# FFN tail of a gated-experts kernel: eight tiles singly and four pairs, each group's product ahead of the next transposes, and the grid subtraction shared by VectorE and TensorE

## What is computed

```python
def _quant_e4m3(t):
    amax = jnp.max(jnp.abs(t)).astype(jnp.float32)
    scale = jnp.maximum(amax / E4M3_MAX, 1e-12)
    fp8 = (t.astype(jnp.float32) / scale).astype(jnp.float8_e4m3fn)
    return (fp8, scale)
...
x = x + jnp.tanh(g_xattn[0]) * _L0_xattn_ref(_layernorm(x, axis=-1), itok_BxS_13_99985, ctx_2048, ctx_2048, ctx_2048)
x = x + jnp.tanh(g_ffn[0]) * _L0_ffn_ref(_layernorm(x, axis=-1), L0_ffn_weight)
```

## Time and profile before

| | us |
|---|---|
| median of 3 runs | 201.29 |
| lowest and highest run | 201.24, 203.76 |
| the profiled execution's own time | 201.43 |
| span of its profile | 199.7 |
| busy in the span: TensorE (PE) | 144.3 |
| VectorE (DVE) | 156.3 |
| ScalarE (ACT) | 112.7 |
| GpSimd (POOL) | 81.8 |

### The profile page before, as it was taken

The page is one execution under the profiler, slowest core; times in us unless marked ns, Lnnn a source line. Parts: engine busy times, 40 slices in busy tenths (PEclk is TensorE's granted clock), DMA queues, the critical chain, the costliest instruction groups (busy, mean ns, idle before and its releaser), DMA issues.

```text
span 199.7 us, 3062 instructions
## 1 busy us (share of the span) xinstructions
PE 144.3 (72%) x723; PEld 69.7 (35%) x727; DVE 156.3 (78%) x351; ACT 112.7 (56%) x166; POOL 81.8 (41%) x117
## 2 busy tenths in 40 slices
PE   0141939998999797999998999999851266566600
PEld 0110424443555343544444445555420223223200
DVE  2876697798758799899989787776686999998820
ACT  2366596887524854688868534233313987666510
POOL 7158787320312344332386673001110023566670
PEclk9999996999999999999999999999997579999985
DMA  0937998200000222111212210000000002132351
GB/s 6 365 113 198 355 408 264 85 2 0 0 3 0 54 56 53 26 39 43 54 26 53 56 26 0 3 0 2 0 5 0 0 0 105 57 153 113 149 208 59
DMA packets 15440, 15.68 MB, mean 79 GB/s; under 512 B 10816, under 2 KB 11328, under 8 KB 15424
## 3 DMA queue, kind: packets, MB, share of 16 engines
q1 hardware_dynamic: 12576, 7.09, 11.8%
q0 software_dynamic: 2560, 8.39, 11.6%
q10 hardware_dynamic: 288, 0.00, 0.1%
HBM read 8.92 MB, written 4.19 MB: 66 GB/s over the span
## 4 chain that ended last, share of the span: by engine, by line
PE 38%; DVE 33%; issue 11%; POOL 7%; ACT 6%; DMA 1%; DVEq 1%; POOLq 0%
PE four_ps L465 10%; PE four_ps L457 10%; PE four_ps L470 9%; DVE w_hi L1044 3%; DVE hT_hi L1052 3%; PE four_ps L498 3%; POOL x L341 3%; PE four_ps L569 2%; DVE bn L880 2%; DVE zT_lo L866 2%; DVE bn L832 2%; DVE x L1056 2%; ACT y L703 2%; DVE z L861 2%; DVE w_lo L824 2%
## 5 line engine op out<-in xcount | busy, mean ns | idle before, releaser
L364 POOL DMA_INDIRECT out<-x,token_of x16 | 19.3, 1208 | 25.4 <-DVE x L1056 22.9
L359 POOL TENSOR_TENSOR rstd<-var,minus_half 128x1 f32<-128x1 f32 x16 | 8.8, 552 | 49.3 <-DVE var L888 49.3
L633 ACT ACTIVATE zT_hi<-four_ps 128x512 f16<-128x512 f32 x19 | 11.3, 595 | 18.9 <-PE four_ps L498 18.9
L457 PE MATMUL four_ps<-w_hi,hT_hi 128*128 x76 | 21.3, 394 | 0.8 <-ACT w_hi L596 0.7
L624 ACT ACTIVATE sg<-four_ps,job_inv_a 128x512 f32<-128x512 f32 x19 | 12.9, 679 | 15.4 <-PE four_ps L470 12.4
L341 POOL DMA_INDIRECT x<-in_x,token_of x16 | 17.4, 1088 | 7.0 <-issue 4.2
L457 PE MATMUL four_ps<-w_hi,zT_hi 128*128 x76 | 19.5, 379 | 0.8 <-ACT zT_hi L633 0.8
L465 PE MATMUL four_ps<-w_lo,hT_hi 128*128 x76 | 19.9, 384 | 0.0
L615 ACT ACTIVATE w<-x,nmr,rstd 128x512 f32<-128x512 f32 x16 | 13.0, 810 | 11.9 <-DVE nmr L894 11.5
L470 PE MATMUL four_ps<-w_hi,zT_lo 128*128 x76 | 19.5, 379 | 0.0
L465 PE MATMUL four_ps<-w_lo,zT_hi 128*128 x76 | 19.5, 379 | 0.0
(11 more groups left out here) (148 smaller groups left out, 293.4 us busy)
## 6 DMA issues: line engine op xcount, KB each, us to landing
w<-in_ctx_t SPq DMA_DIRECT2D x4, 1024.0 KB, 9.4
wf<-in_wf_t SPq DMA_DIRECT2D x1, 512.0 KB, 15.4
x<-in_x,token_of POOLq DMA_INDIRECT x16, 5.9
out<-x,token_of POOLq DMA_INDIRECT x16, 2.9
hT_hi<-h_row SPq DMA_TRANSPOSE x9, 2.3
hT_lo<-h_row SPq DMA_TRANSPOSE x9, 2.3
ids_s<-in_ids SPq DMA_DIRECT2D x1, 8.0 KB, 2.9
g_s<-in_g_x ACTq DMA_DIRECT2D x1, 0.5 KB, 2.7
```

What stands on the lines that cost most here:

```text
L364: pool.indirect_dma_start(out, bass.IndirectOffsetOnAxis(ap=token_of[:, i:i + 1], axis=0), block_of(x1, i), None, bounds_check=T - 1).then ...
L457: pe.matmul(ps, lhs_hi(k), w_block(w_hi, expert, k), start=(k == 0), stop=False)
```

## The change

- `FIRST` makes twelve groups: tiles 0, 1, 2, 3, pairs {4,5}, {6,7}, {8,9}, {10,11}, then 12, 13, 14, 15.
- Transposes go to four f32 banks, `q_ps`, one a tile (tile i to bank i mod 4), and `r_ps`, `c_ps`, `n_ps`, `m_ps` become names of these. The transposes are ordinary matmuls against the identity in place of `pe.transpose`.
- `split(g)` says who subtracts. VectorE rounds tiles 0, 1, 3, 4, 6, 8, 10, 13, 15 as before. For tiles 2, 5, 7, 9, 11, 12, 14 TensorE does it as it transposes: four bf16 matmuls of vm against minus the identity, and four f32 matmuls of vt against the identity, summed in PSUM.
- TensorE issues the transposes of g, waits for their copy, issues the product of g, and only then the transposes of g+1.
- ScalarE scales three groups ahead in place of four, and `to_bf16(g)` follows `copy_qT(g)` in the same turn.
- `max_second` of tile 14 stands ahead of the two end reductions instead of behind them.
- GpSimd makes `minus_ident` at the start; VectorE's `grid` waits for `qT_done` in place of `q8_done` where the ring is used again.

```diff
-        FIRST = [0, 1, 2, 4, 6, 8, 10, 12, 14, 15, TILES]
+        FIRST = [0, 1, 2, 3, 4, 6, 8, 10, 12, 13, 14, 15, TILES]
...
+        q_ps = psum("q_ps", [P, 4 * D], F32)
+        r_ps, c_ps, n_ps, m_ps = [q_ps[:, n * D:(n + 1) * D] for n in range(4)]
...
+        def split(g):
+
+            tiles = list(tiles_of(g))
+            return (tiles[:1], tiles[1:]) if g in (0, GROUPS - 1) or g % 2 or len(tiles) > 1 else ([], tiles)
...
+            pool.tensor_scalar(minus_ident[:, :], ident[:, :], -1.0, None, ALU.mult).then_inc(pool_const, 1)
...
+            def transposed(g):
+
+                by_dve, by_pe = split(g)
+                if reused(g, 4):
+                    pe.wait_ge(qT_copied, reused(g, 4))
+                if by_pe:
+                    pe.wait_ge(vt_done, g + 1)
+                for i in by_pe:
                     for k in range(K):
-                        mm = pe.transpose(qT_ps[g % NQ][:, n * D + k * P:n * D + (k + 1) * P],
-                                          q8[:, i % NB, k * P:(k + 1) * P], ident_bf[:, :])
+                        pe.matmul(q_block(i, k), vm[:, i % NB, k * P:(k + 1) * P], minus_ident[:, :],
+                                  start=(k == 0), stop=False)
+                    for k in range(K):
+                        mm = pe.matmul(q_block(i, k), vt[:, i % NB, k * P:(k + 1) * P], ident[:, :],
+                                       start=False, stop=(k == K - 1))
+                if by_dve:
+                    pe.wait_ge(q8_done, rounded_by(g + 1))
+                for i in by_dve:
+                    for k in range(K):
+                        mm = pe.matmul(q_block(i, k), q8[:, i % NB, k * P:(k + 1) * P], ident_bf[:, :],
+                                       start=(k == 0), stop=(k == K - 1))
                 mm.then_inc(qT_done, 1)
...
-            transpose_q(0)
             for g in range(GROUPS):
-                if g + 1 < GROUPS:
-                    transpose_q(g + 1)
+                transposed(g)
                 pe.wait_ge(qT_copied, g + 1)
...
-            V_AHEAD, Y_BEHIND = 4, 1
+            V_AHEAD = 3
             for g in range(V_AHEAD):
                 scaled(g)
-            for g in range(GROUPS + Y_BEHIND):
-                if g < GROUPS:
-                    copy_qT(g)
+            for g in range(GROUPS):
+                copy_qT(g)
                 if g + V_AHEAD < GROUPS:
                     scaled(g + V_AHEAD)
-                if g >= Y_BEHIND:
-                    to_bf16(g - Y_BEHIND)
+                to_bf16(g)
...
                 if fixed and j == TILES + E:
+                    max_second(j - E - 2)
                     for n, op in enumerate([ALU.max, ALU.min]):
...
             def rounded(g):
 
-                dve.wait_ge(vt_done, g + 1)
-                if reused(g, NB):
-                    dve.wait_ge(qT_done, reused(g, NB))
-                dve.tensor_tensor(ring(q8, g, NB), ring(vt, g, NB), ring(vm, g, NB), ALU.subtract).then_inc(q8_done, 1)
+                for i in split(g)[0]:
+                    dve.wait_ge(vt_done, g + 1)
+                    dve.tensor_tensor(q8[:, i % NB, :], vt[:, i % NB, :], vm[:, i % NB, :], ALU.subtract).then_inc(q8_done, 1)
```

More of the change, by code:

```diff
@@ L67, in gated_experts_kernel @@
         ident_bf = sb("ident_bf", [P, P], BF16)
+        minus_ident = sb("minus_ident", [P, P], BF16)
         below = sb("below", [P, P], F16)
@@ L261, in tiles_of, with rounded_by @@
             return range(FIRST[g], FIRST[g + 1])
+        def split(g):
+            tiles = list(tiles_of(g))
+            return (tiles[:1], tiles[1:]) if g in (0, GROUPS - 1) or g % 2 or len(tiles) > 1 else ([], tiles)
+        def rounded_by(g):
+            return sum(len(split(n)[0]) for n in range(g))
         def ring(t, g, n):
@@ L546, in _, with q_block @@
             pe.matmul(m_ps[:, P:2 * P], ones_f[:, :], diag[:, :], start=True, stop=True).then_inc(xmax_done, 1)
[L548 to L552, removed]
-                    for k in range(K):
-                        mm = pe.transpose(qT_ps[g % NQ][:, n * D + k * P:n * D + (k + 1) * P],
-                                          q8[:, i % NB, k * P:(k + 1) * P], ident_bf[:, :])
+            def q_block(i, k):
+                return q_ps[:, i % 4 * D + k * P:i % 4 * D + (k + 1) * P]
+            def transposed(g):
[5 more added lines that the diff above has]
+                for i in by_pe:
+                    for k in range(K):
+                        pe.matmul(q_block(i, k), vm[:, i % NB, k * P:(k + 1) * P], minus_ident[:, :],
[9 more added lines that the diff above has]
+                                       start=(k == 0), stop=(k == K - 1))
                 mm.then_inc(qT_done, 1)
-            pe.wait_ge(pool_const, 13)
+            pe.wait_ge(pool_const, 14)
             pe.wait_ge(wfq_done, K)
-            transpose_q(0)
             for g in range(GROUPS):
-                if g + 1 < GROUPS:
-                    transpose_q(g + 1)
+                transposed(g)
                 pe.wait_ge(qT_copied, g + 1)
@@ L694, in copy_qT @@
                     act.wait_ge(f_done, reused(g, NF))
-                n = len(tiles_of(g))
-                act.activation(ring(qT, g, NF), qT_ps[g % NQ][:, 0:n * D].rearrange("p (b d) -> p b d", d=D), ACT.Copy)\
+                act.activation(ring(qT, g, NF), ring(q_ps[:, :].rearrange("p (b d) -> p b d", d=D), g, 4), ACT.Copy)\
                     .then_inc(qT_copied, 1)
@@ L961, in job @@
                     w_low(j + 1, [0])
-                if not fixed or j > E + 1:
+                if E + 1 < j < TILES + E:
                     max_second(j - E - 2)
@@ L1036, in grid @@
                 if reused(g, NB):
-                    dve.wait_ge(q8_done, reused(g, NB))
+                    dve.wait_ge(qT_done, reused(g, NB))
                 dve.tensor_scalar(ring(vm, g, NB), ring(v, g, NB), 1.5 * 2.0 ** -6, 2.0 ** 20, ALU.max, ALU.mult)\
```

## The result

The changed kernel takes 210.23 us, the median of 4 runs (207.29 to 210.37), beside 201.94 us for the kernel before (201.24 to 203.76, 4 runs). The ratio is 1.036, 95% interval 1.024 to 1.048: slower. Forecast were 206.2 us, 203.4 to 210.3, and slower.

The account below looks back on a forecast made before the run. VectorE was taken to bound the tail before, 3.99 us a pair; after, a serial TensorE-ScalarE loop of 4.48 us. Stepped by group, the span was 204.6 us; plus 1.73 less 0.14 gave 206.2 us, range 203.4 to 210.3.

Parts of the forecast that it names:

- rival 3: TensorE's tail: weight loads bound the f32 matmuls, 0.19 to 0.22 us a record; +3.9 to +5.6, so 210.1 to 211.8 us; chance 0.12.
- signs of being wrong: VectorE without gaps, f32 records 0.19 us or more apart, clock at 1.2 GHz past 166 or 2.4 before 160, first x_inv moved.
- The loop of a pair: Tail, TensorE and ScalarE in series: transposes, drain, copy, product; 4.48 us a pair against 3.99 before.
- Single tiles: Tail, serial loop of one tile: 2.90 us where TensorE subtracts, 2.32 us where VectorE rounds.
- f32 records: TensorE's added f32 matmuls in the tail: 0.12 us of the array a record, 0.96 us for eight.
- rival 5: TensorE's tail: f32 records as quick as bf16, 56 x 0.065 us less, 203.0 us; chance 0.03.
- Moved and small parts: Tile 14's maximum, ScalarE's last normalisation, GpSimd's minus-identity (some 0.3 us, in idle time) and others: -0.2 to +0.2 us, taken as 0.
- I keep that instant: TensorE's clock in the tail: rises to 2.4 GHz near 162.7 in the changed kernel, as in the kernel before.
- rival 2: Tail: full clock later, near 166.1 or beyond, groups 1 and 2 at half rate; +1.4 to +2.2, 207.6 to 208.4 us; chance 0.15.
- Rival 1: Tail: full clock sooner, near 159.3, from more TensorE work in its first microseconds; 205.3 us; chance 0.15.
- the order is the large term: TensorE's queue in the tail: product ahead of the next transposes waits for its own copy; serial pair 4.48 us against 3.99.
- Rival 4: Tail: VectorE stays the bound and its 2.8 us saving pays, if the copy wait is filled; 198.5 us; chance 0.05.

Follow-up runs that it names:

- the fourth experiment: The changed kernel with 30 idle-time bf16 matmuls, whose result nobody reads, added on TensorE ahead of the tail: 205.45 us, ratio to the kernel before 1.010.

## Why the prediction was right, and where it was off

- *Direction and size.* Slower was forecast, and the range reached to 210.3; the median of 210.23 lies 0.07 us inside it, which is luck. The forecast's own range, 205.0 to 207.5, and the price of every rival but one missed it; that one, rival 3 (210.1 to 211.8), did not happen. One of the signs of being wrong came true, the clock at 1.2 GHz past 166, and the last finish ended at 202.0, not near 198.3. Of the 4.0 us between forecast and measured span, 3.7 were there when the last product started.
- *The loop of a pair*: 4.48 us was worked out, 4.41 measured (179.40, 183.81, 188.22). The copy from f32 took 1.02 us, as from bf16, not 1.11.
- *Single tiles*: 2.90 and 2.32 us forecast; in the chain at the end, from 197.18 to 199.48 is 2.30 for tile 15, and the step to tile 14, whose predecessor's first record is missing, took about 2.9.
- *f32 records*: (1.11 - 0.275) / 7 = 0.119 us apart at full clock (a record is 0.275 long), against 0.12. Their loads last 0.19 us each and don't set the pace, so rival 3 falls, and rival 5 (0.055 us) with it. Rival 5's own sum was off: 56 x 0.065 is 3.6, so 202.6 and not 203.0. The Trainium skill (TensorE: Matmul & The Clock Gate, table Terms) would have it that plain f32 takes four times what the transpose mode does. The nearest rows: the eight records of one tile stand 0.119 apart, so 0.95 us for four f32 matmuls, or 0.24 for each, not 0.44. The four f32 transposes at 61.98 of this trace, which `pe.transpose` made (L454), take 0.60 us, so they stand some 0.11 apart: the plain way costs about twice the transpose, not four times.
- *Moved and small parts*: the tail's first scaling began at 153.79 in place of 153.91, within the bounds given. The minus-identity took GpSimd 0.55 us, not 0.3; it ended at 4.89, and GpSimd was idle for 2.73 us behind it, so it cost nothing.
- *The end*: from the last store's end (203.81) to the span's is 4.8 us, as before. The last store was issued 0.8 us after the finish and took 0.97, where 0.1 and 1.44 were put in: 0.2 us more together.
- *The step that failed* is the clock, "I keep that instant". The rise came at 173.7, not 162.7. That is rival 2, which had a chance of 0.15 and whose price stopped at +2.2 us, with groups 1 and 2 at half rate. My estimate by the same stepping with 173.7, so with group 3 and the transposes of {4,5} at half rate too, is a span of 208.8; 208.6 was measured. By products: tile 2 started 1.2 us later than forecast, tile 3 2.0, the pair {6,7} 3.95, tile 15 3.7, so the loss was complete when the clock rose. I had noted that the gaps for copies were new and still held them against an early rise only. They helped to keep the clock down: with these waits filled it rose at 159.9.
- *Rival 1*, an earlier rise, had 205.3 us; the kernel with the waits filled has nearly this clock (159.9 against 159.3) and took 205.4. The Trainium skill's sentence on the transpose mode (same page, Part 4) pointed to an earlier rise in the changed kernel, where all transposes are ordinary matmuls. The rise came 11 us later, so if that effect exists it was far outweighed; no run separates it.
- *Half right*: "the order is the large term". Undone in the changed kernel it gives back 3.5 us by the lowest runs with idle-time matmuls, but alone in the kernel before it costs only 1.1 us. A pair's serial loop there is 3.5 us and hides under VectorE's 3.99. It is the order together with the f32 work, 1.2 us a pair in the same loop, that passes VectorE's pace.
- *Rival 4*: VectorE's saving pays only when the wait is filled. That condition was the right one: with transposes ahead the shared subtraction makes the kernel 1.3% faster than before, some of it by the clock.

The 8.3 us between the medians are thus, as an estimate, 3.6 us of the loop with the clock nearly full (204.06 less 200.49) and 4.7 us that go with the clock. The two parts are not sharp, since the first compares lowest runs and the whole compares medians. The kernel with the waits filled agrees: the earlier clock alone gave 4.8 us.

## What to carry to other kernels

A wait inside an in-order engine's loop costs nothing as long as the whole loop is shorter than the bounding engine's; work moved onto that loop is paid in full from the moment the loop is longer. So before work goes to an engine that looks idle, add up the loop with every wait and copy in it, and give it something of another group to do in the wait. On TensorE such waits can be paid twice, since they can hold its clock at 1.2 GHz, as they did in this change and did not in the kernel before with the serial order: step the tail with the clock rising late as well as where it rose before.

## What was not expected of the hardware

The clock stayed at 1.2 GHz from about 150 to 173.7 in the changed kernel, with TensorE busy 1.66 to 2.50 of each 2.50 us from 160 to 170. Two added matmuls behind the transposes of each of the first five groups made it rise 13.8 us sooner. A start at full clock didn't always hold either: in the profile of the fourth experiment the clock fell at 158.3, behind a stretch in which TensorE was busy 0.55 of 2.50 us, and rose only near 171.9. And a ScalarE copy of 1024 columns from PSUM takes the same 1.02 us from f32 as from bf16.
